# Decoder stack on one core: the DMA queue's value shifts wait for the scores of the preceding tile, its row shifts for attention products

## The reference

```python
# x: (4, 512, 128); 16 heads of 64; window 32
x = attn_layer(shift_tokens(x), Wqkv[i], q_scale[i], k_scale[i], Wo[i]) + x
x = ffn_layer(shift_tokens(x), ln_g[i], ln_b[i], W1[i], b1[i], W2[i], b2[i]) + x
...
def shift_tokens(t):                   # second half of the features comes from the token before
    a, s = jnp.split(t, 2, -1)
    s = jnp.pad(s, ((0, 0), (1, 0), (0, 0)))[:, :-1]
    return jnp.concatenate([a, s], -1)
def attn_layer(x, Wqkv, qs, ksc, Wo):
    q, k, v = heads of x @ Wqkv
    q, k = l2norm(q) * qs, l2norm(k) * ksc, then rotary with a scale
    # windows of 32 queries see their own 32 keys and the 32 before, masked to a band
    attn = softmax(8 * q @ k^T + mask); out = attn @ v
    return out @ Wo
def ffn_layer(x, ...):                 # layer norm, then a * gelu(gate) with 341 hidden
    a, gate = split(norm(x) @ W1 + b1); return a * gelu(gate) @ W2 + b2
```

## Time and profile before

| | before |
|---|---|
| median of 3 runs | 1852.91 us (1849.08 to 1860.7) |
| profiled execution, its own time | 1859.11 us |
| its span | 1857.1 us |
| granted TensorE clock, mean | 0.95 of full speed |
| TensorE busy | 88% of the span |
| VectorE, ScalarE, GpSimd busy | 76%, 75%, 73% |

### The profile page before, as it was taken

The page is one execution under the profiler, slowest core; times in us unless marked ns, Lnnn a source line. Parts: engine busy times, 40 slices in busy tenths (PEclk is TensorE's granted clock), DMA queues, the critical chain, the costliest instruction groups (busy, mean ns, idle before and its releaser), DMA issues.

```text
span 1857.1 us, 78564 instructions
## 1 busy us (share of the span) xinstructions
PE 1636.3 (88%) x32727; PEld 1374.0 (74%) x32727; DVE 1411.9 (76%) x3127; ACT 1401.4 (75%) x3625; POOL 1359.7 (73%) x971
## 2 busy tenths in 40 slices
PE   6588678989999998998998999999999899989877
PEld 4345447878888877877887888778777778778765
DVE  6678678977788877877887778778877877778751
ACT  4456457887898877878887878878877877788763
POOL 4455467887788877877887878778777877778753
PEclk9889889999999999999999999989999999999998
DMA  3645211112211113111212122122111131112011
GB/s 106 243 159 182 103 48 46 47 36 79 62 51 54 53 40 107 31 56 40 62 54 77 41 57 59 40 79 62 44 53 53 40 98 34 40 39 62 23 31 52
DMA packets 82291, 122.75 MB, mean 66 GB/s; under 512 B 41819, under 2 KB 55316, under 8 KB 81812
## 3 DMA queue, kind: packets, MB, share of 16 engines
q1 hardware_dynamic: 81362, 117.46, 21.2%
q10 hardware_dynamic: 578, 0.26, 0.1%
HBM read 40.81 MB, written 23.41 MB: 35 GB/s over the span
## 4 chain that ended last, share of the span: by engine, by line
PE 74%; issue 8%; ACT 3%; DVE 1%; DMA 0%; SPq 0%; POOL 0%; DVEq 0%; ACTq 0%; POOLq 0%
PE banks L1189 11%; PE banks L1202 10%; PE banks L1107 8%; PE banks L1151 8%; PE banks L1109 7%; PE banks L1108 7%; PE banks L1129 5%; PE banks L1119 4%; PE banks L1164 4%; PE banks L1247 4%; PE banks L1090 2%; PE banks L1219 2%; PE banks L1220 2%; PE banks L1221 2%; ACT f_h L1385 1%
## 5 line engine op out<-in xcount | busy, mean ns | idle before, releaser
L1447 POOL TENSOR_TENSOR qk_c<-qk_c,qk_s 128x1024 f32<-128x1024 f32 x192 | 456.5, 2378 | 110.5 <-DVE qk_s L1544 108.4
L1455 POOL TENSOR_TENSOR qk_c<-qk_c,nrm 128x1024 f32<-128x1024 f32 x192 | 361.8, 1905 | 133.0 <-DVE nrm L1592 133.0
L1349 ACT ACTIVATE prob<-banks,nmax 128x64 f32<-128x64 f32 x1536 | 326.2, 370 | 1.7 <-DVE nmax L1607 1.4
L1533 DVE TENSOR_TENSOR qk_c<-banks,rot 128x512 f32<-128x512 f32 x384 | 262.6, 684 | 54.4 <-ACT sq L1314 52.6
L1107 PE MATMUL banks<-high,xT 128*128 128x512 f32 x576 | 279.7, 486 | 13.1 <-ACT v_own L1322 5.1
L1314 ACT ACTIVATE sq<-banks 128x512 f32<-128x512 f32 x384 | 252.0, 656 | 32.2 <-PE banks L1109 29.1
L1544 DVE TENSOR_TENSOR qk_s<-banks,rot 128x512 f32<-128x512 f32 x384 | 256.6, 668 | 0.0
L1463 POOL TENSOR_TENSOR prob<-prob,pinv 128x512 f32<-128x512 f32 x192 | 196.6, 1045 | 74.7 <-DVE pinv L1622 74.4
L1109 PE MATMUL banks<-high,xT 128*128 128x512 f32 x576 | 235.2, 408 | 1.2 <-issue 1.2
L1108 PE MATMUL banks<-low,xT 128*128 128x512 f32 x576 | 234.2, 407 | 0.7 <-issue 0.7
L1189 PE MATMUL banks<-pT,v_back 64*64 64x32 f32 x6144 | 193.1, 221 | 44.2 <-issue 43.7
(11 more groups left out here) (159 smaller groups left out, 3618.1 us busy)
## 6 DMA issues: line engine op xcount, KB each, us to landing
v_back<-v_own SPq DMA_DIRECT2D x96, 384.0 KB, 3.9
front_raw<-in_L_ffn_Wqkv_dram SPq DMA_DIRECT2D x18, 512.0 KB, 5.5
v_back<-v_own SPq DMA_DIRECT2D x72, 128.0 KB, 2.6
w_high<-high SPq DMA_DIRECT2D x15, 512.0 KB, 2.7
w_low<-low SPq DMA_DIRECT2D x15, 512.0 KB, 4.1
high<-w_high SPq DMA_DIRECT2D x15, 512.0 KB, 4.1
low<-w_low SPq DMA_DIRECT2D x15, 512.0 KB, 4.7
wo<-in_L_ffn_Wo_dram SPq DMA_DIRECT2D x6, 512.0 KB, 5.4
```

Source lines behind the costliest of these rows:

```text
L1349: last = act.activation(prob[:, t % 2, at:at + 64], bank[4 + half][:, 64 * g:64 * g + 64], ACT.Exp, bias=nmax[:, t % 2, 8 * half + g:8 * h ...
L1447: pool.tensor_tensor(x, x, qk_s[:, kind, :], ALU.add).then_inc(s["rotd"], 1)
L1455: pool.tensor_tensor(x, x, bcast(nrm[:, t % 2, HEADS * kind:HEADS * (kind + 1)], 2, DH), ALU.mult).then_inc(s[("qn", "kn")[kind]], 1)
L1533: dve.tensor_tensor(qk_c[:, t % 2, kind, 512 * half:512 * half + 512].rearrange("p (h d) -> p h d", d=DH), bank[n % 2][:, :].rearrange("p ...
```

## The change

Two waits are added on SyncE's queue. `shift_values(t)` waits, besides the stored values of tile t, until the scores of tile t-1 are made (`sc` counts tiles whose scores TensorE has finished; at least t of them). `shift_row(row)` waits, besides the added attention of the row's four tiles, until the attention products of the tile after the row are made (`av` counts tiles; 4 row + 5 of them). `need` leaves out a wait for zero. No instruction of any engine changes its place on its queue.

```diff
 def shift_values(t):
     j = t % GPB
     sp.wait_ge(s["v_r"], 2 * t + 2)
+    need(sp, s["sc"], min(t, TILES))
     if j > 0:
         sp.dma_start(v_back[0:WIN, j, :], v_own[P - WIN:P, j - 1, :]).then_inc(shifted[j], 16)
     sp.dma_start(v_back[WIN:P, j, :], v_own[0:P - WIN, j, :]).then_inc(shifted[j], 16)
...
 def shift_row(row):
     sp.wait_ge(s["added"], GPB * (row + 1))
+    need(sp, s["av"], min(GPB * row + 5, TILES))
     need(sp, s["f3"], row)
```

## The result

| | before | after |
|---|---|---|
| median of the runs on one chip | 1856.81 us (4 runs) | 1910.30 us (4 runs, 1903.8 to 1915.38) |
| ratio, 95% interval | | 1.0285 [1.0226, 1.0344] |
| profiled execution: span | 1857.1 us | 1907.1 us |
| mean granted clock | 0.950 | 0.937 |

The change costs 53 us, or 50.0 by the two profiled spans, where 38 were forecast. The time measured lies 19 us above the number forecast and at the upper end of the range (1910); 4 of these 19 us come from the kernel before, whose median stands at 1856.81 with a fourth run and stood at 1852.91 then.

What follows compares the result with a forecast made beforehand. The prediction took TensorE, without slack, to bound the kernel. Value weights 28.5, query weights 8.8 and clock 8, less 7 gained at code fetches, gave +38 us on the median of 1852.9: 1891 us, range 1866 to 1910.

Steps and rivals of the forecast that it cites:

- What bounds the kernel: TensorE, busy 88% of the span, has no slack, so every microsecond that it stands still is paid.
- (a): At five layer changes, value weights queued behind the last tile's shift delay the fourth projection: net +28.5 us (19.5 to 32).
- (b): Query weights behind the last but one tile's shift delay the new layer's first projection: net +8.8 us (-0.2 to +12.3).
- (c): At layer changes, key weights, Wo and the rotary table load later but are needed later still: no cost.
- (d): FFN weights behind the shift of tile 16l+9 load about 8 us later: no cost, with 1.5 us of cover.
- Row shift, "Cost: none": The row shift goes out later but lands over 4 us before the row statistics read it: no cost.
- Clock: TensorE's granted clock drops behind the new stalls at layer changes: 8 us (0 to 16).
- The gain at code fetches: TensorE's code fetches, mostly in the scores, have fewer transfers beside them: net -7 us (0 to -15).
- The first: Rival: all 58 code waits shorten by 1 us each, giving 13 us faster, 1840 us; chance 3%.
- The second: Rival: weight loads land at their 6.0 us floor and the clock doesn't fall: +9, 1862 us; chance 10%.
- The third: Rival: loads at their ceiling, clock drops after each, FFN columns late: +65, 1918 us; chance 10%.
- The fourth: Rival: the added waits are already met and nothing moves: 1853 us; chance 1%.

Runs made afterwards that it cites:

- e10: Changed kernel without the row-shift wait and with tile 14 of each layer freed from the value-shift wait, so only value weights are late: 1895.54 us, ratio 1.0187.
- e2: Changed kernel without the value-shift wait, so only the row-shift wait is added: 1898.63 us, ratio 1.0243.
- e1: Changed kernel without the row-shift wait, so only the value-shift wait is added: 1914.67 us, ratio 1.0332.
- e4: Changed kernel with the value shift of each layer's last tile (15) freed from its new wait, row-shift wait kept: 1891.36 us, ratio 1.0226.
- e9: Changed kernel without the row-shift wait and with tile 15 of each layer freed from the value-shift wait, so only query weights are late: 1867.14 us, ratio 1.0053.
- e12: Kernel before with 64 no-operations added on TensorE ahead of the rounds, though the trace shows as many instructions as before: ratio 1.0001.
- e5: Changed kernel with both waits kept and the next layer's weights put ahead of the waiting shifts on SyncE's queue: 1842.21 us, ratio 0.9940.
- e11: Changed kernel without the row-shift wait, with the next layer's weights put ahead of the waiting shifts on the queue: 1840.91 us, ratio 0.9924.
- e3: Changed kernel with the value shifts of tiles 14 and 15 of each layer freed from their new wait, row-shift wait kept: 1876.03 us, ratio 1.0128.
- e8: Changed kernel without the row-shift wait and with tiles 14 and 15 of each layer freed from the value-shift wait: 1851.32 us, ratio 0.9960.
- e7: Changed kernel without the row-shift wait; value shifts wait to just before the scores instead, except tiles 14 and 15 of each layer: 1878.67 us, ratio 1.0139.
- e6: Kernel before, without either new wait, with the next layer's weights moved ahead of the shifts on SyncE's queue: 1861.27 us, ratio 1.0045.

## Why the prediction was right where it was, and where it was not

**What bounds the kernel.** Held. TensorE's queue has no slack: what it stood still it paid, and two held loads and the clock behind them make up nearly all of the loss.

**(a) Value weights.** Right in place, mechanism and size: +28.6 us in the third stretch, +28.5 forecast. The single wait is 5.92 where 5.9 was worked out; that it agrees so closely is in part luck, since the chain took 8.0 and not 7.8 us and the work beside it 2.2 and not 2.04. Measured alone (e10) the tile costs 42 us, the stall and what follows it.

**(b) Query weights.** The mechanism was right and the term too small: +12.0 against +8.8. The chain of shift and weights took 8.6 us at tile 48, not 7.8; that is just over the ceiling of 8.5, since the pair landed in 6.3 us, later than the 5.8 of the kernel before. The gain contained in it came as forecast: tile 45 breaks for 1.50 us.

**(c) Key weights, Wo, rotary table; (d) FFN weights.** Right: no wait for them, and lnb in time (issued 917.73, read 922.67).

**Row shift, "Cost: none".** This step was wrong, though the number of the whole change hides it. I asked who reads the row shift and found 4 us of cover; I did not ask what stands behind it on the queue. By itself the row wait costs 2.4% (e2). In the change as a whole it adds nothing that these runs can tell (e1 against the kernel after), because the value wait ends later at the same place.

**Clock.** The term that was mis-sized most. Forecast 8 us; the table has 8.9 + 5.1 = 14.0 in the two stretches that contain no load wait. I had priced the drop by the 28 matmuls of one window, 1.5 us; it lasts longer. Behind (b) it costs 8.9 / 5 = 1.8 us each, and this is firm: the second stretch sums to 47.7 to 48.6 us in every kernel whose query weights come in time, and to 53.2 to 56.9 in the four in which they don't (after, e1, e4, e9). In the same two traces, these 6 us with the 3.2 us of (b) and the 2.4 that the gain fell short make the 12 us between 38 and 50.

Behind (a) the table's 5.1 us is too little. The trace of the kernel before has clock drops in that stretch already (0.80 in two of its five windows, 0.89 in two), more than e12 has with the same stream, so most likely by chance. The sum of the fourth stretch in e12, then in e10:

```profile
sum 67.70, PE 58.87 PEld 48.94 DVE 53.25 ACT 57.96 POOL 44.85; mean PE 11.77 PEld 9.79 DVE 10.65 ACT 11.59 POOL 8.97
```

```profile
sum 84.03, PE 74.18 PEld 63.18 DVE 35.93 ACT 54.42 POOL 19.26; mean PE 14.84 PEld 12.64 DVE 7.19 ACT 10.88 POOL 3.85
```

Besides the kernel before with its 76.1 us, the seven kernels whose value weights come in time (e5 to e9, e11, e12) take 63.6 to 69.8 us there. The three with the row wait alone at that tile (e2, e3, e4) take 74.7 to 78.5, and the three in which the value weights wait for scores (after, e1, e10) 81.2 to 84.0. So the clock behind (a) cost some 11 to 18 us, 2.3 to 3.5 each, and not 0.5: the term as a whole was some 20 to 27 us and not 8. This is also why (a) alone costs 42 us with 28.9 us of waiting, and where a good part of e2's loss lies.

**The gain at code fetches.** Forecast -7 (0 to -15); -7 us by e8 [0.9923, 0.9998], so between -14 and nothing. The -4.6 of the table hangs on the same trace of the kernel before: with e12 in its place the four stretches grow by 63.4 us of 63.0, and next to nothing is left. By the stretches the costs come to some 61 to 68 us, the loss is 53, and so the gain is 8 to 15 (an estimate from these sums). That the forecast came as near as it did is in part luck: a clock term far too small was in part made good by a gain taken too small. The mechanism is supported from both sides (e7, e8, and e6 to e5). Its detail was partly wrong: I named tiles 53, 69 and 85, which should have come down to 1.5 us; the break of 45 did, but theirs did not.

**The rivals.** The first (faster, by 1 us at each code wait) fell: these waits gave back 9.7 us, not 58. The second (floor of the loads, clock that stays up) fell on both counts: 8.0 and 8.6 us, clock 0.81 behind the stall; its sum also takes a gain of 10 us, where the forecast has 7, and gives no reason. The third went too far where it counted late FFN columns and value weights at their ceiling, but its 1918 was nearer to the result than the likeliest 1891: its 12 us for the query weights is what the first stretch shows, and its 14 us for the clock is nearer than 8. The fourth was excluded as said.

## What to carry to other kernels

A wait put on an in-order DMA queue is priced by what stands behind it, not by who reads the transfer that waits: list the prefetches up to the next empty stretch and check each one's due time, for every added wait by itself. Loads whose buffers are already free go ahead of the entry that waits; then a wait that keeps small transfers out of another engine's sensitive stretch can earn something, here 0.4 to 0.8%. Moving the loads alone, without the waits, put them beside a code fetch and cost 0.4% (e6). And a stall of 5 us on TensorE is more than 5 us, since the clock behind it falls too: here by a further 1.8 to 3.5 us each. To size such a term, take more than one trace of the kernel before.

## What the runs showed of the hardware

The code fetch of TensorE was slower with DMA traffic near it: the same breaks sum to 63.6 us when the shifts fly ahead of the scores and to 48.1 when they follow them. With weight loads as well, and no waits, the longest break was 5.2 us (e6). The packet itself takes about as long in each case; it starts later. In the scores of tile 45 the packet that ends the break starts 0.1 us after the scores' first instruction in the kernel after, where no load is in flight, 1.4 us after it in the kernel before and 3.1 us after it in e6; its transfer takes 1.2, 0.9 and 1.2 us, and the breaks are 1.50, 2.48 and 4.63 us.

From e7 to e8 the profiled spans differ by 35.2 us (1878.1 and 1842.9), and both kinds of break together by 17.8. Nearly all the rest is TensorE being busy 15.2 us less (1647.1 and 1631.9) at a granted clock of 0.952 against 0.945; how the breaks lead to the clock was not tried apart.

The Trainium skill (Runtime: NRT & Kernel Launch, Instruction fetch mechanics) says that the fetch is hidden, because instructions are issued more slowly than they are fetched. The measurements differ: in the kernels whose rows stand here the waits at the attention products and in the scores sum to 102 us and more, 20 to 26 of them for ScalarE's exponentials and the rest for code, at fixed places of TensorE's stream.
